# Dense attention's preparation rearranged: value products after the first scores, k's parts on GpSimd, memsets reordered, layer norm in halves

## What is computed

```
def attn(x, Wq, bq, Wk, bk, Wv, bv, Wo, bo, U, V):     # x: layer-normed, 2048 x 128
    q = (x @ Wq.T + bq)  -> 16 heads of 8
    k = (x @ Wk.T + bk)  -> 16 heads of 8
    v = (x @ Wv.T + bv)  -> 16 heads of 8
    zq, zk, zv = q @ V, k @ V, v @ V
    att = softmax(zq @ zk.T / sqrt(rank))               # 2048 x 2048 for each head, no mask
    y   = (att @ zv) @ U.T
    return y (heads side by side) @ Wo.T + bo
```

## Time and profile before

| | us |
|---|---|
| median of 3 runs | 2561.2 |
| lowest and highest | 2557.87 and 2571.74 |
| profiled execution, its own time | 2554.95 |
| profiled execution, span of the records | 2553.1 |
| TensorE busy | 2267.3 (89% of the span) |
| VectorE busy | 2192.4 (86%) |
| ScalarE busy | 2022.9 (79%) |
| GpSimd busy | 1322.4 (52%) |

### The profile page before, as it was taken

How to read it: one execution, slowest core, us unless ns; L and a number is a source line. 1 busy time by engine, 2 the same in 40 slices (tenths; PEclk the granted TensorE clock), 3 DMA queues, 4 the chain that set the end, 5 groups by cost and what they waited for, 6 DMA issues and landing times.

```text
span 2553.1 us, 65940 instructions
## 1 busy us (share of the span) xinstructions
PE 2267.3 (89%) x27383; PEld 1361.1 (53%) x27383; DVE 2192.4 (86%) x2513; ACT 2022.9 (79%) x3616; POOL 1322.4 (52%) x894
## 2 busy tenths in 40 slices
PE   5899999999995788999999899999999999999886
PEld 3122222222223566766776666766666667766664
DVE  6999999999854988989899888889888889988873
ACT  1288777888784688888888888888988889889773
POOL 4111111101003667777777777777776777777650
PEclk8699999999997899999999999999999999999987
DMA  1223222222111100101001100101010100110000
GB/s 38 75 59 92 59 79 70 82 51 64 34 63 47 32 21 10 58 18 26 9 10 60 34 9 10 60 16 26 10 60 16 26 8 10 59 30 19 20 14 17
DMA packets 115166, 95.83 MB, mean 38 GB/s; under 512 B 72118, under 2 KB 89780, under 8 KB 114868
## 3 DMA queue, kind: packets, MB, share of 16 engines
q1 hardware_dynamic: 114516, 91.42, 12.9%
q10 hardware_dynamic: 352, 0.20, 0.1%
HBM read 57.83 MB, written 27.26 MB: 33 GB/s over the span
## 4 chain that ended last, share of the span: by engine, by line
PE 46%; DVE 25%; ACT 19%; issue 9%; POOL 0%; DMA 0%; DVEq 0%; ACTq 0%; SPq 0%; POOLq 0%
PE O_ps L1264 10%; PE E_ps L1256 9%; DVE ss L967 7%; PE B_ps L1367 6%; PE S_ps L1247 5%; DVE mx L923 4%; PE B_ps L1288 4%; PE B_ps L1290 3%; PE B_ps L1289 3%; ACT nrm L686 3%; DVE rs L974 3%; ACT pT L755 2%; ACT pT L753 2%; PE B_ps L1354 2%; DVE tc L1005 2%
## 5 line engine op out<-in xcount | busy, mean ns | idle before, releaser
L670 ACT ACTIVATE PT<-E_ps 128x512 f32<-128x512 f32 x1024 | 534.3, 602 | 186.6 <-PE E_ps L1256 184.9
L923 DVE TENSOR_REDUCE mx<-S_ps 128x1 f32<-128x1024 f32 x512 | 601.3, 1218 | 31.0 <-PE S_ps L1247 25.4
L612 POOL TENSOR_TENSOR tc<-tc,ts 128x1024 f32<-128x1024 f32 x96 | 229.2, 2387 | 240.3 <-DVE ts L1017 240.3
L1247 PE MATMUL S_ps<-KS,QS 48*128 48x512 bf16 x1024 | 326.7, 403 | 30.1 <-DVE mx L923 22.1
L1256 PE MATMUL E_ps<-QS,KS 64*128 64x512 bf16 x1024 | 318.0, 387 | 4.7 <-ACT PT L670 4.6
L548 POOL CAST w_cut_b<-w_raw_b 128x512 fp32r<-128x512 f32 (+1 forms) x48 | 27.6, 574 | 550.7 <-DMA w_raw_b<-in_Wqkv 413.5
L570 POOL TENSOR_TENSOR pr<-pr,mxB 128x1024 f32<-128x1024 f32 x96 | 182.8, 1904 | 241.0 <-DVE mxB L1056 241.0
L1288 PE MATMUL B_ps<-w_qkv,x_cut 128*128 128x512 f32 x576 | 263.5, 457 | 33.0 <-issue 16.6
L967 DVE TENSOR_REDUCE ss<-nrm 128x16 f32<-128x1024 f32 x192 | 227.9, 1215 | 69.4 <-ACT nrm L686 69.3
L1264 PE MATMUL O_ps<-PT,va 128*32 128x512 f32 x2048 | 278.3, 616 | 0.0
L1314 PE MATMUL B_ps<-ident,tc 128*128 128x128 f32 x1536 | 216.2, 290 | 64.1 <-ACT o_T L727 56.3
(11 more groups left out here) (199 smaller groups left out, 4679.4 us busy)
## 6 DMA issues: line engine op xcount, KB each, us to landing
Wqkv_cut<-w_cut_b SPq DMA_DIRECT2D x72, 256.0 KB, 2.4
w_qkv<-Wqkv_cut SPq DMA_DIRECT2D x36, 512.0 KB, 5.6
rot<-in_rot SPq DMA_DIRECT2D x96, 128.0 KB, 2.5
w_raw_b<-in_Wqkv SPq DMA_DIRECT2D x36, 256.0 KB, 3.0
W_cut<-w_cut_b SPq DMA_DIRECT2D x24, 170.5 KB, 2.7
w<-W_cut SPq DMA_DIRECT2D x12, 341.0 KB
QS<-zp_q SPq DMA_DIRECT2D x96, 32.0 KB
w_o<-in_Wo SPq DMA_DIRECT2D x6, 512.0 KB, 4.2
```

The costliest lines, as they stand in the source:

```text
L670: e.activation(m.PT[n % NPT][:, :], turns.bank("probs", n)[:, :], ACT.Exp).then_inc(turns.sem("probs", n), 1)
L923: e.tensor_reduce(m.mx[h % 2][:, i, hf:hf + 1], m.S_ps[n % 2][:, :, :], AX.XY, ALU.max).then_inc(s["sc_max"], 1)
L1247: mm = e.matmul(m.S_ps[n % 2][:, c, :], m.QS[sl][rows, i * P:(i + 1) * P], m.KS[sl][rows, k:k + CH], start=True, stop=True)
```

## The change

The layer norm works on two halves of 8 token tiles. x comes in two DMAs ahead of the identity. The squares are made by ScalarE (a new instruction for each half) instead of VectorE, and the mean of the squares and the epsilon are added in one instruction. GpSimd clears QS and KS first; `va` is cleared at the end of its preparation, after the stream copies and the parts of k. The z products alternate, k then q for each chunk, and start when the first chunk of turned x is out. Of k's four steps VectorE keeps the first (line 925 of the changed kernel); GpSimd does the other three (lines 549 to 553). VectorE's bf16 cast of the identity comes after the parts of q. The value products leave the preparation: one chunk is made after each second step of head 0 (after u = 1, 3, 5, 7). ScalarE issues the DMAs for KS of head 0 ahead of its copies into `va`.

```
-    e.memset(m.va[:, :, :, :], 1.0).then_inc(s["zeroA"], 1)
...
+    for g in range(NC):
+        z, zp = m.z["k"][:, chunk_cols(g)], [m.zp["k"][:, i, chunk_cols(g)] for i in range(PARTS)]
+        w.wait_ge(s["skew"], 2 * NC)
+        w.wait_ge(s["part_k"], 3 * g)
+        w.wait_ge(s["z_k"], g + 1)
+        e.tensor_copy(zp[1], z).then_inc(s["part_k"], 1)
+        w.wait_ge(s["part_k"], 3 * g + 1)
+        e.tensor_tensor(z, z, zp[1], ALU.subtract).then_inc(s["part_k"], 1)
+        w.wait_ge(s["part_k"], 3 * g + 2)
+        e.tensor_copy(zp[2], z).then_inc(s["part_k"], 1)
+    w.wait_ge(s["part_k"], 3 * NC)
+    e.memset(m.va[:, :, :, :], 1.0).then_inc(s["zeroA"], 1)
```

ScalarE and VectorE:

```
+    for i in range(2):
+        half = slice(i * NT // 2, (i + 1) * NT // 2)
+        w.wait_ge(s[f"lnA{i}"], 3)
+        e.activation(m.sq[:, half, :], m.x_tok[:, half, :], ACT.Square).then_inc(s[f"sqA{i}"], 1)
...
-    w.wait_ge(s["lnA"], 3)
-    e.tensor_tensor(m.sq[:, :, :], m.x_tok[:, :, :], m.x_tok[:, :, :], ALU.mult).then_inc(s["lnA"], 1)
...
+    for g in range(NC):
+        c = chunk_cols(g)
+        w.wait_ge(s["z_hi"], 2 * g + 1)
+        e.scalar_tensor_tensor(out=m.z["k"][:, c], in0=m.banks[(5 + 2 * g) % 8], scalar=m.b_z["bk"][:, 0:1], in1=m.zp["k"][:, 0, c],
+                               op0=ALU.add, op1=ALU.subtract).then_inc(s["z_k"], 1)
+        z, zp = m.z["q"][:, c], [m.zp["q"][:, i, c] for i in range(PARTS)]
+        w.wait_ge(s["z_hi"], 2 * g + 2)
+        e.scalar_tensor_tensor(out=z, in0=m.banks[(6 + 2 * g) % 8], scalar=m.b_z["bq"][:, 0:1], in1=zp[0], op0=ALU.add,
+                               op1=ALU.subtract).then_inc(s["part"], 1)
+        w.wait_ge(s["part"], 4 * g + 1)
+        e.tensor_copy(zp[1], z).then_inc(s["part"], 1)
+        w.wait_ge(s["part"], 4 * g + 2)
+        e.tensor_tensor(z, z, zp[1], ALU.subtract).then_inc(s["part"], 1)
+        w.wait_ge(s["part"], 4 * g + 3)
+        e.tensor_copy(zp[2], z).then_inc(s["part"], 1)
+    w.wait_ge(s["ld_id"], 16)
+    e.tensor_copy(m.ident_bf[:, :], m.ident[:, :]).then_inc(s["idb"], 1)
```

TensorE, in the loop over u (`dense_values(g)` is the chunk of value products as it was):

```
+        if u < 2 * NC and u % 2:
+            dense_values(u // 2)
+        if u == 2 * NC:
+            w.wait_ge(s["va"], NC)
```

More of the change, by code:

```diff
@@ L336, in wait_part_a @@
     w.wait_ge(s["ld_o1"], 16 * NC * H)
-    w.wait_ge(s["part"], 8 * NC)
+    w.wait_ge(s["part"], 4 * NC)
+    w.wait_ge(s["part_k"], 3 * NC)
     w.wait_ge(s["idb"], 1)
@@ L861, in vector_a @@
 def vector_a(e, w, m, s):
-    w.wait_ge(s["ld_id"], 16)
-    e.tensor_copy(m.ident_bf[:, :], m.ident[:, :]).then_inc(s["idb"], 1)
     mean, var = m.stat[:, 0, :], m.stat[:, 1, :]
     c, t, r = m.stat[:, 2, :], m.stat[:, 3, :], m.stat[:, 4, :]
[L866 to L872, removed]
-    w.wait_ge(s["lnA"], 3)
-    e.tensor_tensor(m.sq[:, :, :], m.x_tok[:, :, :], m.x_tok[:, :, :], ALU.mult).then_inc(s["lnA"], 1)
[L875 to L880, removed]
+    halves = [slice(i * NT // 2, (i + 1) * NT // 2) for i in range(2)]
+    wide = lambda a: a.unsqueeze(2).to_broadcast([P, NT // 2, P])
+    for i, hf in enumerate(halves):
+        x = m.x_tok[:, hf, :]
+        w.wait_ge(s[f"ld_x{i}"], 16)
+        e.tensor_reduce(mean[:, hf], x, AX.X, ALU.add).then_inc(s[f"lnA{i}"], 1)
+        w.wait_ge(s[f"lnA{i}"], 1)
+        e.tensor_scalar(mean[:, hf], mean[:, hf], 1.0 / P, None, ALU.mult).then_inc(s[f"lnA{i}"], 1)
+        w.wait_ge(s[f"lnA{i}"], 2)
+        e.tensor_tensor(x, x, wide(mean[:, hf]), ALU.subtract).then_inc(s[f"lnA{i}"], 1)
+    for i, hf in enumerate(halves):
+        w.wait_ge(s[f"sqA{i}"], 1)
+        e.tensor_reduce(var[:, hf], m.sq[:, hf, :], AX.X, ALU.add).then_inc(s[f"lnA{i}"], 1)
+    w.wait_ge(s["lnA0"], 4)
+    w.wait_ge(s["lnA1"], 4)
+    e.tensor_scalar(c, var, 1.0 / P, 1e-5, ALU.mult, ALU.add).then_inc(s["rA_arg"], 1)
     w.wait_ge(s["rA_exp"], 1)
@@ L1221, in tensor_a, with dense_values @@
     w.wait_ge(s["fold"], 8)
-    w.wait_ge(s["xT"], NC)
[L1223 to L1226, removed]
-            e.matmul(m.banks[(5 + NC * i + g) % 8], m.w_z[n][:, :], m.xn_T[:, chunk_cols(g)], start=True, stop=True).then_inc(s["z_mm"], 1)
-    w.wait_ge(s["const"], 2)
-    for g in range(NC):
-        w.wait_ge(s["part"], 4 * g + 1)
-        bank = m.banks[(5 + g) % 8]
+    for g in range(NC):
+        w.wait_ge(s["xT"], g + 1)
+        for i, n in enumerate(("Wk", "Wq")):
+            b = (5 + 2 * g + i) % 8
+            if 1 <= b <= NC:
+                w.wait_ge(s["xT"], b)
+            e.matmul(m.banks[b], m.w_z[n][:, :], m.xn_T[:, chunk_cols(g)], start=True, stop=True).then_inc(s["z_mm"], 1)
+    def dense_values(g):
+        bank = m.banks[4 + g]
+        w.wait_ge(s["const"], 2)
         for j in range(4):
@@ L1236, in tensor_a @@
         mm.then_inc(s["v_mm"], 1)
-    w.wait_ge(s["part"], 8 * NC)
-    w.wait_ge(s["va"], NC)
+    w.wait_ge(s["part"], 4 * NC)
+    w.wait_ge(s["z_k"], NC)
     turns = ExpTurns(m, s)
```

61 lines of the change are left out of this document (25 added, 36 removed).

## The result

| | before | after |
|---|---|---|
| median of 8 runs each, us | 2560.7 | 2574.31 |
| lowest and highest | 2555.58 and 2571.74 | 2569.04 and 2583.44 |
| profiled execution, span of the records | 2553.1 | 2580.2 |
| first score starts | 63.42 | 54.55 |
| end of head 0's last reduce | 102.1 | 115.4 |

The ratio after to before is 1.0056, with a 95% interval of 1.0034 to 1.0078: the change made the kernel 13.6 us slower in the medians. 2577.8 was predicted, with a range of 2562 to 2587. The moment by which the prediction measured everything, the end of head 0's last reduce, came 13.3 us later; 16.6 was predicted.

What follows compares the result with a forecast made beforehand. It took the whole effect as the shift of the moment when head 0's maxima are complete (102.1 us before). First score −5.0 and head 0 +21.6 gave +16.6; 2561.2 + 16.6 = 2577.8 us, range 2562 to 2587.

Steps and rivals of the forecast that it cites:

- F: Moment when the folded Wo is out of PSUM, 24.38 us in the kernel before; predicted at about 20.3.
- the mark: End of head 0's last maximum reduce, 102.1 us before; predicted at 118.7.
- Layer norm: F comes at about 20.3.: Ahead of the z products: half-size operations, VectorE's last tensor_scalar meeting GpSimd's memsets; folded Wo out 4.1 us earlier.
- Parts: q is ready at F + 31.7.: Parts of k and q: VectorE and GpSimd hold each other, 4.8 us a chunk; q's last cast waits for `va`'s memset.
- rival D: Parts: the engines hold each other, but q's last cast slips in ahead of the memset; +10.3, 2571.5; chance 0.12.
- the same six DMAs take the same: From q's last part to head 0's first score: six DMAs last as before, 6.4 us; score at 58.4, 5.0 earlier.
- Head 0 with the value products inside: +21.6 us.: Head 0: chunks of value products at clock 0.50 leave VectorE waiting 5.4 us more, four times, 21.6.
- B: Head 0: the clock rises while values and scores alternate, 8.4 us for four cycles; +3.4, 2564.6; chance 0.11.
- C: Parts: GpSimd and VectorE don't hold each other, parts end at F + 18.6; +3.5, 2564.7; chance 0.13.
- E: Parts and head 0: B and C together, first score at 45.3; −9.7, 2551.5; chance 0.06.

## Why the prediction was right, and where not

The time of the whole was right to 3.5 us, and the two steps that decide the sign were right. Two terms between them were wrong by more than that, with opposite signs.

| term | predicted | measured |
|---|---|---|
| folded Wo out (F) | 20.3 | 21.29 |
| F to q's last part | 31.7 | 22.80 |
| q's last part to the first score | 6.4 | 10.46 |
| first score | 58.4 | 54.55 |
| first score to the mark | 60.3 | 60.9 |
| the mark | 118.7 | 115.4 |
| against before | +16.6 | +13.3 |

**Layer norm: F comes at about 20.3.** Right in mechanism. I had 19.4 or 21.2 and took the middle; it was the later one, 21.29, in this and every other run with these memsets. (Half of 2.29 is 1.15 and not the 1.23 that I gave for half of x; the trace of the change has 1.22.)

**Parts: q is ready at F + 31.7.** Wrong by 8.9 us. 6.3 of it is rival D: the last cast slipped in ahead of the memset, to which I gave 0.12. The other 2.6 is the period of a chunk, 4.08 (4.31 for the first) instead of 4.8. The step that failed is "its cast and its product (1.9 us) cover VectorE's q step (0.74) and then hold q's first cast by 1.2 us". A wait ends with the one GpSimd instruction that is in progress, and VectorE gets in before the next one. In the second chunk VectorE's first cast came at 33.18, GpSimd's cast ended at 33.23, and VectorE's cast took its own 0.43: it did not wait for GpSimd's product. In the nine traces in which GpSimd makes k's parts, q's first cast of a chunk took 0.43 to 0.83 and never the 1.6 that I had stepped through.

It looks as if the 0.05 us between these two moments had decided the order for all that follows. The other runs speak against it. In four of the nine traces GpSimd was ahead in the second chunk, as in the run with the values back ahead of the scores:

```profile
31.98 0.61 DVE L932 CAST zp_q<-z_q 128x512 bf16<-128x512 f32 x1
...
33.64 1.26 DVE L936 CAST zp_q<-z_q 128x512 bf16<-128x512 f32 x1
...
36.25 0.43 DVE L932 CAST zp_q<-z_q 128x512 bf16<-128x512 f32 x1
```

Such a chunk took 4.27 us, 0.2 more, and the third and fourth chunks came out alike in all nine. So did the end: VectorE's last product holds GpSimd's last cast (0.95 instead of 0.61), GpSimd comes to its memset 0.49 or 0.50 us after q's last cast was asked for, in each of the eight traces in which the memset follows at once. Rival D was therefore the regular outcome of this order and not a rare one. That the engines hold each other was right for both sides, GpSimd's too, for which the trace of before had no row.

**First score: "the same six DMAs take the same".** Wrong by 4.1. In the kernel before, SyncE was reading other heads' rows when ScalarE loaded KS of head 0. In the change the parts of k and q are ready within 0.3 us of each other (43.80 and 44.09), both queues read the same eight partitions, and that costs 3.2 of the 4.1, shown by the run with other source rows. The rest is open.

**Head 0 with the value products inside: +21.6 us.** Right: 22.1, in four gaps of 5.52 or 5.53 (5.4 predicted). The runs show it from both sides: with the values ahead of the scores there is no gap, and with the values moved alone they are all there.

**Rivals.** B is out: the clock stayed at 0.50 until 128, with TensorE busy 37.36 of the 40 us from 62 to 102. The Trainium skill, TensorE: Matmul & The Clock Gate, Part 1, has sustained work release the throttle; this trace does not agree for this mix, and in the run with the gap filled the clock even fell within it. C and E are out: the engines do hold each other. D's mechanism happened, but D's time, 2571.5, left out the DMAs' 4.1 us. So the sign and the greater part of the size came from a mechanism that was right, the gaps; that the median came within 3.5 us of my number was in part luck, because the parts (8.9 too long) and the DMAs (4.1 too short) cancelled by half.

The mark moved by 13.3 and the medians by 13.6, so taking the effect on the whole from the shift of that one moment held here.

## What to carry to other kernels

Work moved behind a shallow buffer is hidden only if a piece of it, with the producer's own work, is shorter than the consumer's work on what is buffered. Count it at the clock that the engine really has there, and cut it fine if it must be there, or leave it where the engine is idle anyway. Fine pieces helped here by 8.5 us of 22.1, and the idle place by all of it. When a transfer's duration is taken from an old trace, look at which partitions the other queue was reading at that time; making two inputs ready at the same moment can put both their transfers on the same rows. A wait found harmless is so only behind the present schedule: the identity's cast cost nothing until the DMAs were made faster, and 1.3 us then.

## What the runs showed of the hardware that I had not expected

- Two queues that read the same eight partitions at once slow each other: six DMAs of 32 KB took 5.71 us to issue instead of 4.18, and the last landed after 5.63 instead of 3.44, with only one side's source rows changed.
- GpSimd is held by VectorE as VectorE is by GpSimd: its cast took 0.95 instead of 0.61, a 6.94 memset 7.08. A cast of VectorE that waited got in between two instructions of GpSimd that were 0.06 us apart (in the run with the values ahead of the scores, where it was asked for at 31.98, GpSimd's casts end and begin at 32.31 and 32.37, and the second took 0.69 instead of 0.61). The order in the first two chunks differed between runs; the last two were the same in all nine traces.
- TensorE's granted clock fell from 1.00 to 0.50 at about 59.4 in the run with the filled gap, in a chunk of value products, after TensorE had been busy for 28.1 of the 30 us from 30 to 60 (19.76 and 8.30 in the windows); its pauses lay among the scores, from 54.2 to 57.6.
